# Two overlapped blocks for keys, queries, values and statistics ahead of a quantised cross-attention

## The reference

```python
x = x + xattn(layernorm(x), ctx)          # then self-attention, then the experts
q = (x @ Wq + bq) ; kv = cond @ Wkv + bkv ; k, v = kv[:, :, 0], kv[:, :, 1]   # 16 heads of 16
q = fq_sym(q / 4, axis=-1)                # step = max|.| over the head's 16 values / 127
k = fq_sym(k, axis=-1)
v = fq_sym(v, axis=2)                     # step = max|.| over all 8192 rows, per column
# fq_sym: clip(round(x / step), -127, 127) * step, with step at least 1e-8
attn = fq_unsigned(softmax(q @ k.T)) ; out = (attn @ v) @ Wp + bp
```

## Time and profile before

| | us |
|---|---|
| median of 3 runs | 6527.99 (6514.9 to 6553.14) |
| profiled execution | 6548.42, its span 6546.9 |
| DVE busy in the span | 5643.9 |
| ACT busy | 4741.1 |
| PE busy | 4634.3 |
| POOL busy | 4506.7 |
| block 4 begins (first xn) | 232.2 |
| block 5 begins (v_amax) | 350.2 |
| block 6 begins (v_op fill) | 423.6 |

### The profile page before, as it was taken

The page is one execution under the profiler, slowest core; times in us unless marked ns, Lnnn a source line. Parts: engine busy times, 40 slices in busy tenths (PEclk is TensorE's granted clock), DMA queues, the critical chain, the costliest instruction groups (busy, mean ns, idle before and its releaser), DMA issues. The chain is left out here.

```text
span 6546.9 us, 142949 instructions
## 1 busy us (share of the span) xinstructions
PE 4634.3 (71%) x49686; PEld 2154.8 (33%) x49686; DVE 5643.9 (86%) x7682; ACT 4741.1 (72%) x6485; POOL 4506.7 (69%) x3196
## 2 busy tenths in 40 slices
PE   6736666667766666666676666666666646769999
PEld 3412222222222222222222222222222233454555
DVE  7579999999999999999999999999999955872222
ACT  3329999999898898888898899999899843331111
POOL 1238888888888898888888888888898833420000
PEclk9769999999999999999999999999999978979999
DMA  3138777777777777777777777777777730010000
GB/s 119 51 73 143 139 144 143 142 140 143 141 143 137 138 147 137 136 143 140 138 138 143 140 140 142 146 139 143 139 140 143 141 99 4 0 35 3 6 6 10
DMA packets 2231970, 735.70 MB, mean 112 GB/s; under 512 B 2175779, under 2 KB 2209412, under 8 KB 2225573
## 3 DMA queue, kind: packets, MB, share of 16 engines
q1 hardware_dynamic: 2196261, 576.08, 43.4%
q0 software_dynamic: 35456, 157.33, 13.9%
HBM read 168.97 MB, written 27.26 MB: 30 GB/s over the span
## 5 line engine op out<-in xcount | busy, mean ns | idle before, releaser
L804 DVE TENSOR_SCALAR_CACHE_REDUCE scores<-ring,step 128x2048 f32<-128x2048 f32 (+2 forms) x2560 | 4782.2, 1920 | 70.4 <-PE ring L731 58.0
L863 ACT ACTIVATE n_op<-scores,bias 128x2048 uint8<-128x2048 f32 x2048 | 4076.2, 1997 | 285.5 <-DVE m_rest L811 285.4
L679 POOL CAST nT<-pairs 128x2048 f16<-128x2048 uint8 x2048 | 3791.4, 1890 | 532.5 <-DMA pairs<-n_op 513.3
L731 PE MATMUL ring<-x_all,q_op 128*128 128x512 bf16 x8192 | 2225.4, 385 | 676.5 <-DVE scores L804 585.7
L731 PEld LDWEIGHTS ring<-x_all,q_op 128*128 128x128 bf16 x8192 | 682.7, 98 | 1881.7 <-DVE scores L804 1180.0
L728 PE MATMUL ring<-x_all,q_op 128*128 128x512 bf16 x2048 | 633.0, 391 | 725.3 <-DVE scores L804 709.0
L743 PE MATMUL pO<-nT,v_op 128*32 128x128 f16 x32768 | 662.0, 224 | 157.0 <-ACT att_g L881 111.2
L743 PEld LDWEIGHTS pO<-nT,v_op 128*32 128x32 f16 x32768 | 484.3, 98 | 607.5 <-issue 512.1
L728 PEld LDWEIGHTS ring<-x_all,q_op 128*128 128x128 bf16 x2048 | 116.8, 97 | 997.8 <-DVE scores L804 979.3
L863 ACT ACTIVATION_READ_ACCUMULATOR n_op<-scores,bias 128x1 f32 x2048 | 396.0, 193 | 0.0
L1642 DVE TENSOR_TENSOR h_up<-h_gate,pUp 128x512 f32<-128x512 f32 x112 | 77.0, 687 | 298.1 <-ACT h_gate L1631 298.1
(11 more groups left out here) (195 smaller groups left out, 3553.0 us busy)
## 6 DMA issues: line engine op xcount, KB each, us to landing
x_all<-keys_transposed POOLq DMA_DIRECT2D x128, 768.0 KB, 8.6
v_st<-value_integers POOLq DMA_DIRECT2D x128, 256.0 KB, 3.5
pairs<-n_op SPq DMA_TRANSPOSE x2048, 2.8
keys_transposed<-kT_s POOLq DMA_DIRECT2D x32, 384.0 KB, 3.5
x_all<-in_x SPq DMA_DIRECT2D x2, 4096.0 KB, 14.9
cT<-in_ctx_T SPq DMA_DIRECT2D x32, 256.0 KB, 3.0
q_op<-queries_transposed POOLq DMA_DIRECT2D x384, 16.0 KB, 8.4
value_integers<-v_int SPq DMA_DIRECT2D x1, 4096.0 KB, 12.2
```

What stands on the lines that cost most here:

```text
L679: nc.gpsimd.tensor_copy(nT[par][:, j * EK:(j + 1) * EK, :].rearrange("p (a c) b -> p a c b", c=2), src).then_inc(s_un, 1)
L731: mm = nc.tensor.matmul(slot(t, j)[:, n * BANK:(n + 1) * BANK], q_op[b][:, t * P:(t + 1) * P], k_op[b][:, at + n * BANK:at + (n + 1) * BAN ...
L804: nc.vector.tensor_scalar(score[t % 2][:, at:at + width * BANK], slot(t, j)[:, 0:width * BANK], step[b][:, t:t + 1], None, ALU.mult, ALU.m ...
L863: nc.scalar.activation(n_op[par][:, j * EW:(j + 1) * EW], score[par][:, j * EW:(j + 1) * EW], ACT.Exp, bias=bias[par][:], scale=-1.0, accu ...
```

## The change

The five blocks become three. Block 1 loads only wkv_sb and the biases, and SP doesn't wait for them; the loads of x_all, wq_sb and wp_sb go into the key block behind the first two context tiles. The query bias is split into 16-bit parts together with the key and value biases (b_all, b_parts are 768 wide), and in the query block the bias product is a 16-bit one with 128 contraction rows.

In the key block DVE's `quantise` ends with the requantised key k_a (buffered twice). ScalarE makes the first and second 16-bit part by casts (`first_part`, `second_part`), GpSimd the remainders by subtraction (`first_remainder`, `second_remainder`); the links of one key pair are spread over neighbouring iterations. PE runs three projections ahead. DVE also takes bn_stats of one x tile per iteration and, per pair of iterations, the maximum over four value tiles and a running maximum v_amax; aggregation, square root and reciprocal follow the loop.

In the query block all buffers are doubled, loops are written out, PE multiplies after it has transposed further tiles. The value steps and the eight portions of rounding sit between DVE's queries: steps after iteration 1, portions after iterations 3 to 10; the value store is issued behind the query store of iteration 11. What is left of the value block is the zero fill, a quarter on GpSimd and three quarters on DVE.

```diff
             def _(sp):
-                sp.dma_start(x_all[:], x_t).then_inc(s_x, 16)
...
+                weights(wkv_sb, a["L0_xattn_Wkv"], s_wkv)
+                sp.wait_ge(s_zero, 1)
                 for r in range(PARTS):
...
-                sp.wait_ge(s_w, 7 * 16)
-                sp.wait_ge(s_x, 16)
...
-        layer_norm("query")
...
                 load(0, 0)
                 load(1, 1)
+                sp.dma_start(x_all[:], x_t).then_inc(s_x, 16)
+                for dst, src in ((wq_sb, a["L0_xattn_Wq"]), (wp_sb, a["L0_xattn_Wp"])):
+                    sp.dma_start(dst[:], src.rearrange("(c p) n -> p c n", p=P)).then_inc(s_wq, 16)
...
+                def first_remainder(it, i):
+                    pool.wait_ge(s_k0, after(it))
+                    pool.sem_inc(s_zero, 1)
+                    nc.gpsimd.tensor_tensor(heads(k_b[i][:]), heads(k_a[i][:]), part(i, 0), ALU.subtract).then_inc(s_kd, 1)
+
+                def second_remainder(it, i):
+                    pool.wait_ge(s_k1, after(it))
+                    pool.sem_inc(s_zero, 1)
+                    nc.gpsimd.tensor_tensor(part(i, 2), heads(k_b[i][:]), part(i, 1), ALU.subtract).then_inc(s_kp, 1)
...
+                with pool.Fori(0, NI // 2 - 1) as k:
                     for i in range(2):
                         it = k * 2 + i
...
+                        second_remainder(it + 1, 1 - i)
+                        store(it, i)
+                        first_remainder(it + 2, i)
...
-                with pe.Fori(0, NI // 2 - 1) as k:
+                project(2, 1, 0)
+                with pe.Fori(0, NI // 2 - 2) as k:
                     for i in range(2):
                         turn(k * 2 + i, i)
-                        project(k * 2 + i + 2, k + 1, i)
+                        project(k * 2 + i + 3, k + 1 + i, 1 - i)
...
+                def first_part(it, i):
+                    act.wait_ge(s_kq, after(it))
+                    act.wait_ge(s_ktp, after(it - 2))
+                    nc.scalar.copy(part(i, 0), heads(k_a[i][:])).then_inc(s_k0, 1)
+
+                def second_part(it, i):
+                    act.wait_ge(s_kd, after(it))
+                    nc.scalar.copy(part(i, 1), heads(k_b[i][:])).then_inc(s_k1, 1)
...
+                with act.Fori(1, NI // 2 - 2) as k:
                     for i in range(2):
-                        evacuate(k * 2 + i, i, k)
-                        copies(k * 2 + i + 2, i)
...
+                        it = k * 2 + i
+                        second_part(it + 1, 1 - i)
+                        evacuate(it, i, k)
+                        copies(it + 3, 1 - i)
+                        first_part(it + 2, i)
...
+                    link(nc.vector.tensor_tensor(heads(k_s[:]), k, spread(k_rst[:]), ALU.mult))
+                    link(nc.vector.tensor_scalar(k_r[:], k_s[:], ROUND, ROUND, ALU.add, ALU.subtract))
+                    dve.wait_ge(s_kd, after(it - 2))
+                    nc.vector.tensor_tensor(heads(k_a[i][:]), heads(k_r[:]), spread(k_st[:]), ALU.mult).then_inc(s_kq, 1)
...
+                def value_maximum(k):
+                    dve.wait_ge(s_vc, after(2 * k + 1))
+                    dve.wait_ge(s_vm, 2 * k + 1)
+                    nc.vector.tensor_reduce(v_four[:], v_f[:, bass.ds(k * 2 * G, 2 * G), :].rearrange("p t c -> p c t"),
+                                            AX.X, ALU.max, apply_absolute_value=True).then_inc(s_vm, 1)
+                    dve.wait_ge(s_vm, 2 * k + 2)
+                    nc.vector.tensor_tensor(v_amax[:], v_amax[:], v_four[:], ALU.max).then_inc(s_vm, 1)
...
-                        nc.tensor.matmul(pQ[:, g, :], ones[0:1, :], bq_sb[:], start=True, stop=False)
+                        nc.tensor.matmul(pQ[i][:, g, :], ones_h[:], b_parts[:, 2 * D:3 * D], start=True, stop=False)
...
+                for it in range(NI_Q):
+                    queries(it)
+                    if it == V_FIRST + 1:
+                        value_steps()
+                    if V_FIRST + 3 <= it < V_FIRST + 3 + KT // VB:
+                        round_values(it - V_FIRST - 3)
```

397 lines of the change are left out of this document (231 added, 166 removed).

## The result

The changed kernel takes 6433.1 us in the median of 4 runs (6425.7 to 6443.6), beside it the kernel before 6521.4 (6502.5 to 6553.1, 4 runs). The ratio is 0.986, with a 95% interval of 0.9827 to 0.9893: 88 us or 1.4% faster. Forecast were 6428, within 6385 to 6475.

A forecast was written before the change was run, and what follows sets the result against it. DVE was taken to bound the key and value blocks, PE the query block. The attention loop would start at 213 + 106 + 4.5 = 323.5 us against 423.6, so 6528 - 100 = 6428 us, range 6385 to 6475.

The forecast's parts named there:

- Part 1: Start: x load behind two context tiles; first key product at 11 us, steady pairs from 31, gaining about 23.
- Part 2: Key loop: four DVE operations move away, but waits for GpSimd leave 5.68 us per iteration, 170 us for 15 pairs.
- The layout in time: Key loop: DVE and GpSimd operations placed in time, iterations of 5.25 and 6.1 us, pair 11.35 us.
- the copies' row: Earlier self-attention stage: DVE copies of 0.19 us take 0.97 beside GpSimd two-input products, taken as sign of a lock.
- Part 3: Drain from the last quantise to the key block's end: 12 us, ending at 213 us against 232.2.
- Part 4: Query block: 16-bit bias shortens PE's iteration, value work lies between queries; 106 us against 118.
- Part 5: Value block goes except the zero fill: 4.5 us with a barrier, against 73.4.
- (4): Rival, key loop: slow GpSimd remainders on the interleaved layout; at 4.5 us each, 6587 us; chance 0.03.
- (2): Rival, key loop: the lock costs more as stalls chain, 6.7 us per iteration, 6459 us; chance 0.18.
- (5): Rival: x load holds the first pairs, values' rounding adds to a DVE-bound query block; 6455 us; chance 0.05.
- (3): Rival: query block at either bound, 13 us less or 12 more, 6415 or 6440 us; part of each case.
- (1): Rival, key loop: the lock costs little, loop at ScalarE's 5.1 us, 17 us less, 6411 us; chance 0.22.

The follow-up runs named there:

- the experiment on TensorE's order: Changed kernel with key product 3 set ahead of the first transposition in TensorE's order, and each later product likewise: 6431.3 us.
- that experiment: Changed kernel with GpSimd's two remainders cut from 512 to 16 columns, the smaller key parts left out for all heads but one: 6410.7 us.

## Why the prediction was right, point by point

**The total.** 95.6 us by the marks and 88 by the medians against 100. The single terms were not all as good as their sum, and that the sum came within 5 us is in part luck: the terms too small add up to 23 us, those too large to 19.

| part | predicted | measured |
|---|---|---|
| start, to the third key reduction | 31 | 30.5 |
| 15 pairs from there | 170 | 182.4 (to 212.9) |
| drain | 12 | 10.5 |
| fill of the query block | 9.3 | 10.1 |
| three plain query iterations | 17 | 10.8 |
| value steps and eight value iterations | 53.5 | 52.4 |
| plain iterations behind them | 22 | 12.7 |
| tail | 4 | 11.8 |
| zero fill, barrier | 4.5 | 6.8 |

The rows of the query block are cut at starts of reductions, which don't fall where the forecast cut. The value steps (2.0 us) stand in the row of the three plain iterations: these took 2.9, 4.9 with the steps, and 3.1. The row of plain iterations behind holds four in the measurement, for five in the forecast; the fifth took 2.7 and stands in the tail.

**Part 1** was right in size (30.50) and in mechanism: the context reload behind x held product 2 until 24.15 against the 24 forecast, and ScalarE's copies(2) ahead of second_part(0) held the first transposition. But I let the steady pairs begin right there. The first pair took 18.9 us (30.50 to 49.38), since the chain that I had named goes on: remainders, transposition, product 3, copy. That is 7.2 us over a steady pair and the larger half of the loop's excess of 12.4. Of the 7.2 us 5.96 are the wait for product 3, which the experiment on TensorE's order traced to the orders of two engines; the other 1.3 are waits for GpSimd, 3.4 us in this pair against 2.16 in a steady one. Part 1 also left out that PE comes back from its wait for the context at a granted clock of 0.52, which cost 1.5 us. (The 7.79 us in the earlier trace rows that the prediction names are the duration of SP's issue of the weights, not its distance from the load of x.)

**Part 2** was right where it mattered most. The layout in time gave 11.35 us per pair, 11.66 were measured; 15 x 0.31 = 4.7 us. The waits had been put at 1.9 us a pair, and are 2.16, shown by taking their cause away. The layout counts from the end of one quantise to the end of the next, and so counted it was met closely: the iteration without a value reduction had 5.25 us forecast and takes 5.25 (123.53 to 128.78, the ends of the products L382), with 0.6 and 1.0 us of waiting forecast and 0.89 and 0.84 measured; the other had 6.1 and takes 6.41, with a wait of 0.3 forecast and 0.43 measured. (From one key reduction to the next they look like 3.97 and 7.69, since the value reduction then falls into the second.) Two durations were a little short: the value reduction 1.92 for 1.73, which was a sixteenth of one over all 64 tiles, and GpSimd's remainders 1.15 and 1.26 in the median for 1.04. DVE's own sum of 4.8 us per iteration was right: with the waits gone the pair took 9.50, 4.75 per iteration. ScalarE's chain of 5.1 as a floor stays open: it holds one remainder of 1.04, which is 0.2 to 0.44 in that experiment, so its floor there would be some 4.4, below DVE, and no kernel with whole remainders ran its loop under 5.5 us per iteration.

**The row of the normalisation.** In the earlier trace rows q_a, beside GpSimd's one-input normalisation, loses at most 0.25 us, and I took that as a sign against the lock. It is none for the key loop, whose GpSimd operation is the two-input subtraction, and the layout rightly went by the copies' row. But it isn't chance either. In the kernel before, where the second of two normalisations runs from 245.01 to 246.23 us:

```profile
243.81 2.42 POOL L358 TENSOR_SCALAR xn<-x_all,mean_var,rstd 128x256 f32<-128x256 f32 x2 [5.49 <-PE pX L372]
...
245.19 0.91 DVE L439 TENSOR_TENSOR q_a<-q_f,q_rst 128x512 f32<-128x512 f32 x1
```

q_a starts 0.2 us into a normalisation; a wait to its end would make it 1.73 us long, and it takes 0.91. Another q_a of that kernel starts 0.5 us into a normalisation (325.00 in 324.51 to 325.73) and takes 0.69, as it does alone; so does one of the changed kernel (246.15 in 245.42 to 246.64). The profile's spans on GpSimd are rough, but no q_a of either kernel takes more than 0.94 us, whatever it starts in. The other way round there is a wait. Timeline of the changed kernel, two normalisations beside a value product:

```profile
249.00 2.29 DVE L595 TENSOR_TENSOR v_f<-v_f,v_rst 128x2048 f32<-128x2048 f32 x1
250.24 3.99 POOL L463 TENSOR_SCALAR xn<-x_all,mean_var,rstd 128x256 f32<-128x256 f32 x2 [0.65 <-PE pX L476]
```

and the durations of all 32:

```profile
L463 POOL TENSOR_SCALAR xn<-x_all,mean_var,rstd x32: 1208/1218/4236, 223.4 to 292.8; 128x256 f32<-128x256 f32 x32
```

The first of the two takes 2.79 us instead of 1.22 and ends at 253.03, 0.25 us behind the rounding that follows the product (251.32 to 252.79). The three longest (3.57, 3.57 and 4.24 us) likewise end 0.24 or 0.25 us behind a rounding. So GpSimd's normalisation is held by VectorE's products and roundings, and VectorE's products aren't held by the normalisation. The Trainium skill, "SBUF — State Buffer", section "SBUF: two separate sides", has it that whoever starts first gets the pair for the whole instruction, for a VectorE operation with two SBUF inputs against any GpSimd operation that reads SBUF. The two-input subtraction of the key loop agrees; the normalisation, which reads SBUF too, doesn't, and there the measurement decides. Why the two differ isn't shown.

**Part 3**, the drain, came out at 10.5 us for 12, counted from the end of the last pair; counted as its working was, from the end of the last quantise (210.4), it is 13.0, of which 2.5 lie beside the last value reduction. ScalarE's square root stands behind two evacuations (at 219.07) and the block ends with the store that was issued at 218.06, as laid out.

**Part 4** came out at 97.8 us for 106, and three terms of it were mis-sized. I had put the plain iterations at 5.7 us for half clock, and 4.5 for between: the first ones took 2.9 to 3.1 and the last five 3.1 in the mean, since the clock rose to 1.00 in the first 15 us; in the experiment with the float32 bias it stayed at 0.50 for the first 27. That is some 15 us gained. (The bias products were put at 0.2 us and 0.3 at most; they take 0.27 at the high clock and 0.42 at the low one.) In the other direction the tail: 9.1 us behind DVE's last work, for 4. I had written that the value store lies under the queries and that the query stores behind it are only wanted at the end. They are wanted earlier, by ScalarE's buffers, and the end of the block waits for them. Part 4 named SP's wait in front of the last four stores, but not the 12 us of transfer in front of them on the same queue. The value iterations at 6.3 us were right (6.5).

**Part 5**: VectorE's fill of 6144 columns takes 5.18 us where I had put 3.3, judged by its small memsets; 2.3 us in all with what follows it.

**The rivals.** (4), slower by slow remainders, is out: 1.15 and 1.26 us per remainder against the 3.4 that it needed at the least (4.7 by ScalarE's chain). (2) is out with a pair of 11.66 against 13.4. (5) is partly there: the x load does hold the first pair. (3) had the block at 93 to 118 us, and it was 97.8. (1) put the loop at ScalarE's 5.1 and less waiting than laid out; there was more of it.

## What to carry to other kernels

When work moves from VectorE to GpSimd, lay both out in time and charge each VectorE product, scalar operation or rounding with the rest of a two-input GpSimd operation beside it, even a small one over 32 numbers: this layout met the loop within 3%, and moving the work was still worth 10 us. Look in the trace for the very GpSimd operation that you plan, as a one-input normalisation didn't hold VectorE's products. Put VectorE's reductions and reciprocals beside GpSimd's operations, and expect that removing a waiting operation moves its wait to the next one. For a store on a shared queue ask not when its data are wanted, but who waits for the buffers of the stores behind it.

## What the runs showed of the hardware

Not expected were: a query stage with one-row float32 bias products (0.58 us mean, two per tile) at 0.50 of the clock from 222 to 250 us, with PE busy 10.0 of 10 us from 230 on, where the 16-bit form has 1.00 from 235 to 250; a GpSimd normalisation stretched from 1.21 to 4.24 us by VectorE's products and roundings, while a product that started inside a normalisation lost 0.25 us at most; and fills of float32 zeros at 0.84 ns per column on VectorE (5.18 us for 6144, 3.47 for 4096), about the rate of GpSimd's (3.51 for 4096), so that an even split between the two is the better one (4.65 us from fill to heads block for 6.79).
